# Four-layer convolution block: weights of two mixing steps in one transfer, spectra as the stationary operand, single buffers, results stored by image, weight preparation split over three engines

## What is computed

```
x_ft = jnp.fft.rfft2(x, norm='ortho')
xt = x_ft[:, :, :56, :57]
w = jax.lax.complex(weight[:, :, :56, :57, 0], weight[:, :, :56, :57, 1])
out_ft = jnp.einsum('bchw,cohw->bohw', xt, w)
...
return jnp.fft.irfft2(out_ft_full, s=(H, W), norm='ortho')
```

## Time and profile before

| | |
|---|---|
| Time, median of 3 runs | 11767.94 us (11765.45 to 11776.15) |
| Time of the profiled execution | 11769.75 us |
| Its span | 11767.7 us |
| Mixing stage, first matmul to last | 1629.3 to 2627.4 us |
| Busy in the span | PE 88%, DVE 67%, ACT 51%, POOL 33% |

### The profile page before, as it was taken

The page is one execution under the profiler, slowest core; times in us unless marked ns, Lnnn a source line. Parts: engine busy times, 40 slices in busy tenths (PEclk is TensorE's granted clock), DMA queues, the critical chain, the costliest instruction groups (busy, mean ns, idle before and its releaser), DMA issues.

```text
span 11767.7 us, 292004 instructions
## 1 busy us (share of the span) xinstructions
PE 10317.4 (88%) x120871; PEld 9151.4 (78%) x120871; DVE 7890.7 (67%) x13708; ACT 5969.8 (51%) x7016; POOL 3941.8 (33%) x3304
## 2 busy tenths in 40 slices
PE   7989978874999889999999999999889999999996
PEld 5777777774888878888888888888778888888885
DVE  7777722115677777777777777777677777777775
ACT  4666621112555555555555555555555555555553
POOL 0000000002444444444444444444444444444442
PEclk9999988886999999999999999999999999999996
DMA  8999999982111121111111111111121111111100
GB/s 206 239 241 241 245 210 233 235 214 53 28 39 36 44 45 36 36 37 37 39 36 39 36 39 37 39 39 36 42 46 37 36 36 38 36 39 38 37 22 17
DMA packets 1001966, 947.34 MB, mean 81 GB/s; under 512 B 592800, under 2 KB 937872, under 8 KB 980944
## 3 DMA queue, kind: packets, MB, share of 16 engines
q1 hardware_dynamic: 972048, 708.59, 28.4%
q0 software_dynamic: 28608, 220.21, 5.0%
HBM read 605.77 MB, written 322.96 MB: 79 GB/s over the span
## 4 chain that ended last, share of the span: by engine, by line
PE 38%; DVE 17%; ACT 7%; issue 7%; POOL 5%; DMA 1%; SPq 0%; DVEq 0%; POOLq 0%; ACTq 0%
PE c_ps L1029 24%; PE c_ps L1100 3%; POOL c_cube L1740 3%; PE c_ps L1178 3%; PE c_ps L1113 2%; PE c_ps L1165 2%; DVE c_v L1542 2%; ACT c_xp L1286 2%; DVE c_xp L1506 2%; DVE c_bn L1486 2%; DVE c_s L1605 2%; DVE c_xr L1524 2%; ACT c_sq L1349 1%; ACT c_xp L1226 1%; DVE c_qt L1580 1%
## 5 line engine op out<-in xcount | busy, mean ns | idle before, releaser
L1029 PE MATMUL c_ps<-c_xp,c_wst 128*128 128x224 f16 x45696 | 4911.4, 265 | 154.8 <-DVE c_xp L1506 154.8
L1029 PEld LDWEIGHTS c_ps<-c_xp,c_wst 128*128 128x128 f16 x45696 | 4366.7, 98 | 634.9 <-issue 415.6
L1715 POOL TENSOR_TENSOR c_xr<-c_sm,c_xr 128x448 f32<-128x448 f32 x448 | 704.0, 1572 | 2217.0 <-DVE c_xr L1524 2216.9
L1740 POOL TENSOR_TENSOR c_cube<-c_sq,c_qk 128x896 f32<-128x896 f32 x448 | 928.3, 2093 | 1194.3 <-ACT c_sq L1340 1194.3
L1317 ACT ACTIVATE c_qt<-c_ps 128x896 f32<-128x896 f32 x224 | 205.8, 919 | 2042.1 <-PE c_ps L1121 2042.1
L1275 ACT ACTIVATE c_tn<-c_xr,c_nrm 64x448 f32<-64x448 f32 (+1 forms) x832 | 956.0, 1153 | 57.0 <-DVE c_xp L1506 27.0
L1100 PE MATMUL c_ps<-c_wqkv,c_xn 64*128 64x192 f32 x6272 | 791.2, 367 | 200.5 <-DVE c_v L1542 193.0
L619 PE MATMUL b_ps<-b_xs,b_wt 64*64 64x64 f32 x6384 | 774.2, 294 | 207.0 <-DVE b_xj L595 160.8
L1286 ACT ACTIVATE c_xp<-c_tn 128x1080 f16<-128x1080 f32 (+1 forms) x544 | 572.2, 1063 | 737.4 <-DVE c_tn L1499 733.6
L1506 DVE TENSOR_TENSOR c_xp<-c_tn,c_xp 128x1080 f16<-128x1080 f32 (+1 forms) x544 | 664.1, 1230 | 271.7 <-ACT c_xp L1286 270.7
L1100 PEld LDWEIGHTS c_ps<-c_wqkv,c_xn 64*128 64x128 f32 x6272 | 516.3, 195 | 384.5 <-DVE c_v L1542 287.2
(11 more groups left out here) (158 smaller groups left out, 17750.2 us busy)
## 6 DMA issues: line engine op xcount, KB each, us to landing
b_wt<-in_L_conv_weight SPq DMA_DIRECT2D x56, 2048.0 KB, 21.8
a_xc<-in_x SPq DMA_DIRECT2D x64, 1568.0 KB, 21.4
x<-a_x1s POOLq DMA_DIRECT2D x64, 1568.0 KB, 12.1
a_xh<-x SPq DMA_DIRECT2D x64, 1568.0 KB
c_xr<-x SPq DMA_DIRECT2D x224, 448.0 KB, 4.0
out<-c_xr SPq DMA_DIRECT2D x448, 224.0 KB, 3.1
b_xs<-xf SPq DMA_DIRECT2D x28, 2048.0 KB, 24.5
yf<-b_ys POOLq DMA_DIRECT2D x28, 2048.0 KB, 12.1
```

Of the source, the lines that this page charges most:

```text
L1029: ins = pe.matmul(sums(c, p), wst[:, ws, pr, FIRST_TAP[p] + k].rearrange("p q o -> p (q o)"), xp[:, xs, PLANE[kind] + f, row:row + CROWS, ...
L1715: pool.tensor_tensor(here, apart(sm[:, half]).unsqueeze(1).to_broadcast([P, 2, CROWS, QW]), here, ALU.add).then_inc(s.added, 1)
L1740: pool.tensor_tensor(cube[:, :, k].rearrange("p q r c -> p r q c"), sq[:, :, :, k], qk[:, :, :, k], ALU.mult).then_inc(done, 1)
```

## The change

- The weights of two steps (`m`, 14 pairs) come in one transfer for each half: 4.2 MB with pieces of 1024 bytes. `wt` still has two buffers, each now of two steps. For that the rows of a step are re-numbered (a permutation of the constant `fwd_h`; the amount of work is the same).
- The spectra `xs` have one buffer. `load_x(k)` waits until `turn` has read the spectra before (`turned`), and stands in SP's program behind the weights of its pair.
- `turn` makes three parts (minus imaginary, real, imaginary) for each frequency with the images innermost, `xt`, with three DVE instructions that read `xs` in steps of 512 bytes and write without gaps. `xt` has two buffers.
- PE takes 64 columns of `xt` as the stationary operand, and the 64 outputs' weights, 1024 bytes apart, as the moving one. Number and sizes of the matmuls are the same.
- The results `ys` are laid out by output channel and have one buffer: the copies of step k + 1 wait for the stores of step k. A step is stored with four transfers of 32 partitions (32 images, 16 KB each) into `yf`, now (image, real or imaginary, frequency row, channel, 64). The places of two neighbouring images are 1792 KB apart there.
- Stage C loads an image's mixed spectra with two transfers without gaps, half the bytes of before, and `ys` is half as large.
- In `prepare_weights` ACT makes the high f16 part, and DVE the low one; of the 8 slices of `spread` DVE makes 5 (125 instructions), and POOL 3, with 49 instructions of 384 elements.

SP's program in the mixing stage, before: one step of the loop's body, two transfers of weights (L528) and one of spectra (L531); a row "ISA" in front holds the waits.

The diff, without the parts that only rename:

```diff
-        wt = sb("wt", [P, 2, C, FP // 2, 2])
-        xs = sb("xs", [P, 2, B, FP // 2, 2])
-        xj = sb("xj", [P, 2, B, FP // 2, 2])
-        ys = sb("ys", [P, 2, B, FP // 2, 2])
-        loaded = [sem("loaded0"), sem("loaded1")]
+        wt = sb("wt", [P, 2, C, 2, FP // 2, 2])
+        xs = sb("xs", [P, B, FP // 2, 2])
+        xt = sb("xt", [P, 2, KW, 3, B])
+        ys = sb("ys", [P, C, FP // 2])
+        w_loaded = [sem("w_loaded0"), sem("w_loaded1")]
+        x_loaded = sem("x_loaded")
         turned = sem("turned")
         mixed = [sem("mixed_low"), sem("mixed_high")]
         copied = [sem("copied_low"), sem("copied_high")]
-        stored = [sem("stored0"), sem("stored1")]
+        stored = sem("stored")
         padded = sem("padded")
-        PER = min(BANK // (2 * B), 8)
+        PER = BANK // C
         GROUPS = -(-KW // PER)
         block = ctx.enter_context(nc.Block())
         @block.sync
         def _(sp):
-            def load(k, odd):
-
+            def load_w(m, odd):
                 for half in range(2):
-                    if above_zero((k - 1) * GROUPS):
-                        sp.wait_ge(mixed[half], (k - 1) * GROUPS)
+                    if above_zero((m - 1) * 2 * GROUPS):
+                        sp.wait_ge(mixed[half], (m - 1) * 2 * GROUPS)
                         sp.nop(nofuse=True)
-                src = weight.rearrange("c o (k two) w r -> two k c o w r", two=2)
+                src = weight.rearrange("c o (m two u) w r -> two m c o u w r", two=2, u=2)
                 for half in range(2):
-                    sp.dma_start(wt[C * half:C * half + C, odd],
-                                 src[half, bass.ds(k, 1)].rearrange("k c o w r -> (k c) o (w r)")
-                                 ).then_inc(loaded[odd], 16)
-                sp.dma_start(xs[:, odd], xf[bass.ds(k, 1)].rearrange("k p b f -> (k p) (b f)")).then_inc(loaded[odd], 16)
-
-            load(0, 0)
-            load(1, 1)
-            with sp.Fori(0, KP // 2 - 1) as t:
+                    sp.dma_start(wt[C * half:C * half + C, odd].rearrange("p o u w r -> p o (u w r)"),
+                                 src[half, bass.ds(m, 1)].rearrange("m c o u w r -> (m c) o (u w r)")
+                                 ).then_inc(w_loaded[odd], 16)
+
+            def load_x(k):
+                if above_zero(k):
+                    sp.wait_ge(turned, k)
+                    sp.nop(nofuse=True)
+                sp.dma_start(xs[:], xf[bass.ds(k, 1)].rearrange("k p b f -> (k p) (b f)")).then_inc(x_loaded, 16)
+
+            load_w(0, 0)
+            load_x(0)
+            load_w(1, 1)
+            for k in range(1, 4):
+                load_x(k)
+            with sp.Fori(0, KP // 4 - 1) as t:
                 for odd in range(2):
-                    load(2 * t + (2 + odd), odd)
+                    load_w(2 * t + (2 + odd), odd)
+                    for u in range(2):
+                        load_x(4 * t + (4 + 2 * odd + u))
         @block.gpsimd
...
             pool.memset(ys[:], 0.0).then_inc(padded, 1)
-            def store(k, odd):
+            def store(m, u):
+                k = 2 * m + u
                 for half in range(2):
                     pool.wait_ge(copied[half], (k + 1) * GROUPS)
                     pool.nop(nofuse=True)
-                pool.dma_start(yf[bass.ds(k, 1)].rearrange("k p b f -> (k p) (b f)"), ys[:, odd]
-                               ).then_inc(stored[odd], 16)
+                for half in range(2):
+                    for r in range(2):
+                        rows = slice(C * half + B * r, C * half + B * r + B)
+                        there = yf[:, r, bass.ds(4 * m + (2 * half + u), 1)]
+                        pool.dma_start(there.rearrange("b k o w -> (b k) (o w)"), ys[rows].rearrange("p o w -> p (o w)")
+                                       ).then_inc(stored, 16)
             store(0, 0)
-            store(1, 1)
+            store(0, 1)
             with pool.Fori(1, KP // 2) as t:
-                for odd in range(2):
-                    store(2 * t + odd, odd)
-            for odd in range(2):
-                pool.wait_ge(stored[odd], 16 * (KP // 2))
+                for u in range(2):
+                    store(t, u)
+            pool.wait_ge(stored, 64 * KP)
         def take(eng, copy, half, between):
...
             def body(k, odd):
-                if above_zero(8 * (k - odd)):
-                    eng.wait_ge(stored[odd], 8 * (k - odd))
+                if above_zero(64 * k):
+                    eng.wait_ge(stored, 64 * k)
                 for g in range(GROUPS):
                     lo, hi = g * PER, min(g * PER + PER, KW)
                     eng.wait_ge(mixed[half], k * GROUPS + (g + 1))
-                    copy(ys[C * half:C * half + C, odd, :, lo:hi].rearrange("p b w r -> p w b r"),
-                         ps[C * half:C * half + C, 4 * half + g % 4, 0:2 * B * (hi - lo)].rearrange(
-                             "p (w b r) -> p w b r", b=B, r=2)).then_inc(copied[half], 1)
+                    rows = slice(C * half, C * half + 2 * B)
+                    copy(ys[rows, :, lo:hi].rearrange("p o w -> p w o"),
+                         ps[rows, 4 * half + g % 4, 0:C * (hi - lo)].rearrange("p (w o) -> p w o", o=C)
+                         ).then_inc(copied[half], 1)
                     if g == GROUPS // 2:
...
             def turn(k, odd):
-                dve.wait_ge(loaded[odd], 24 * (k + (2 - odd)))
+                dve.wait_ge(x_loaded, 16 * (k + 1))
                 for half in range(2):
                     if above_zero((k - 1) * GROUPS):
                         dve.wait_ge(mixed[half], (k - 1) * GROUPS)
-                dve.tensor_scalar(xj[:, odd, :, 0:KW, 0], xs[:, odd, :, 0:KW, 1], -1.0, None, ALU.mult)
-                dve.tensor_copy(xj[:, odd, :, 0:KW, 1], xs[:, odd, :, 0:KW, 0]).then_inc(turned, 1)
+                by_freq = xs[:, :, 0:KW].rearrange("p b w r -> p r w b")
+                dve.tensor_scalar(xt[:, odd, :, 0], by_freq[:, 1], -1.0, None, ALU.mult)
+                dve.tensor_copy(xt[:, odd, :, 1], by_freq[:, 0])
+                dve.tensor_copy(xt[:, odd, :, 2], by_freq[:, 1]).then_inc(turned, 1)
...
         def _(pe):
-            def body(k, odd):
-                pe.wait_ge(loaded[odd], 24 * (k + (2 - odd)))
+            def body(m, odd, u):
+                k = 2 * m + u
+                pe.wait_ge(w_loaded[odd], 16 * (m + (2 - odd)))
                 pe.wait_ge(turned, k + 1)
                 for g in range(GROUPS):
                     lo, hi = g * PER, min(g * PER + PER, KW)
@@ -612,20 +631,24 @@
                             pe.nop(nofuse=True)
                     for f in range(lo, hi):
-                        at = 2 * B * (f - lo)
-                        for r, src in ((0, xs), (1, xj)):
+                        at = C * (f - lo)
+                        for r in range(2):
                             for half in range(2):
                                 rows = slice(C * half, C * half + C)
-                                ins = pe.matmul(ps[rows, 4 * half + g % 4, at:at + 2 * B], wt[rows, odd, :, f, r],
-                                                src[rows, odd, :, f], start=(f == lo and r == 0),
+                                ins = pe.matmul(ps[C * half:C * half + 2 * B, 4 * half + g % 4, at:at + C],
+                                                xt[rows, u, f, 1 - r:3 - r].rearrange("p r b -> p (r b)"),
+                                                wt[rows, odd, :, u, f, r], start=(f == lo and r == 0),
                                                 stop=(f == hi - 1 and r == 1), skip_group_check=True)
                                 if f == hi - 1 and r == 1:
                                     ins.then_inc(mixed[half], 1)
-            body(0, 0)
-            body(1, 1)
-            with pe.Fori(1, KP // 2) as t:
+            def step(t):
                 for odd in range(2):
-                    body(2 * t + odd, odd)
+                    for u in range(2):
+                        body(2 * t + odd, odd, u)
+
+            step(0)
+            with pe.Fori(1, KP // 4) as t:
+                step(t)
...
+SPREAD_DVE = 5
...
+        def turned_taps(ky):
+            return ps[0:C, 3 * (ky % 2):3 * (ky % 2) + 3].rearrange("c b x -> c (b x)")[:, 0:TAPS * C].rearrange(
+                "c (k o) -> c k o", k=TAPS)
+
+        def place(part, ky, q):
+            pr, rp = divmod(ky + q, 2)
+            return to["wst"][C * rp:C * rp + C, part, pr, :, q]
...
+            pool.wait_ge(loaded, 16 * len(LOADS))
+            pool.nop(nofuse=True)
+            shape = [P, WS - SPREAD_DVE, P]
+            for t in range(25):
+                there = to["spread"][:, SPREAD_DVE:WS]
+                here = there if t == 0 else term[:]
+                pool.tensor_tensor(here, taps[:, t].unsqueeze(1).to_broadcast(shape),
```

(38 more changed lines are left out.)

5 lines of the change are left out of this document (4 added, 1 removed).

## The result

The changed kernel takes **11,731.8 us** (median of 10 runs, 11,718.8 to 11,739.6) against 11,764.1 of the kernel before, measured beside it: ratio 0.9972, 95% interval 0.9963 to 0.9980. It is 0.28% faster. The forecast was 11,805, slower; the time lies in the forecast's range (11,700 to 11,950), the sign was wrong.

What follows compares the result with a forecast made beforehand. The prediction took the mixing stage's transfer queue, empty during `turn`, as the bound: +79 there, -28 preparation, -3.5 and -10 at C's start, +37 us on 11769.75, giving 11,805 us (range 11,700 to 11,950).

Steps and rivals of the forecast that it cites:

- for later images these loads have nobody waiting: Stage C: the halved loads of spectra save time only for image 0 (10 us), nothing for later images.
- the rest of C at nothing: Stage C behind its start: no term in the sum, so no change of time expected.
- `turn` at 8.6 us: Mixing stage, once a pair: three instructions take 8.6 us (lower bound 3.4) with the queue empty; a pair takes 75.7.
- the first rival: Mixing stage: `turn` costs 3.4 us, total put at 11,728 us; decides from about 5.5 us downwards; chance 32%.
- Start and end of the stage: Mixing stage: first `turn` at 1648.0 us, step 1's to 1709.1, step 26 at 2642, end 2717 against 2638.2.
- Copies at nothing: Mixing stage: copies into `ys` with gaps, even at twice their time 1.4 us of a group's 4.0, hidden.
- Stores: Mixing stage rival: stores land after 18.6 us, each us over 24.6 costs two a pair; 11,911 us at 29; chance 15%.
- the pace of 126 ns: PE in the mixing stage: a pair of records in one half keeps 126 ns, between half and double that.
- The rival of a dear moving operand: PE in the mixing stage: gaps cost double, a step takes 57.6 us, PE is the bound, total 12,376; chance 8%.
- Preparation, -28: Weight preparation: split -11 us, `spread` -19, and 2 added for DVE and POOL at once, 28 us shorter.
- The term of 2 us for DVE and POOL at once: Weight preparation: 2 us added for both engines working in SBUF at the same time.
- Start of C, -13.5: Start of stage C: halved memset of `ys` saves 3.5 us, halved spectra of image 0 save 10.

Runs made afterwards that it cites:

- `code_back`: The changed kernel with 111 idle instructions more in PE's program, in the weight preparation: 11,773.3 us, 1.0005 of the kernel before.
- `turn_long`: The changed kernel with the third instruction of `turn` run three times over: 11,788.4 us, 1.0018 of the kernel before.
- `pool_later`: The changed kernel with POOL's share of `spread` starting only when DVE has laid out the kernel's parts: the preparation stage takes 119.5 us.
- `spread_undone`: The changed kernel with all of `spread` on DVE again, the split still with ACT: the preparation stage takes 123.6 us, 5.3 more than the changed kernel.

## Why the prediction was wrong

- **The step that failed** is "for later images these loads have nobody waiting", and with it the rest of C at nothing. It is true of the loads: with the same light loads, `code_back` has the old 8941.3 us. But the change also makes the program of PE's mixing loop twice as long and so moves all of stage C in its pieces of 256 instructions: 52 us in the two profiles, 34 to 39 against the other kernels with that PE program, and by the medians some 40 (`code_back` 11,773 against 11,732). No term of the sum spoke of it, although the kernel before has waits for nothing else ("issue") in its rows. That the time lies in the range is luck: `turn` (-45), the conflict of DVE and POOL (+10) and C (-41) together take the sum of 11,805 to 11,729, and a range made for `turn` and the stores happened to be wide enough.
- **`turn` at 8.6 us**: it took 5.1, between my bounds of 3.4 and 8.6, and close below the 5.5 from which I had the first rival decide (cheap `turn`, faster). But that rival did not bring the gain either: with `turn` at 5.1 the sum is 45 us lower, 11,760, which is no difference. That "faster" came out is, for this rival, luck. The mechanism was right: with the very 8.6 us I had assumed (`turn_long`) a pair takes 76.3 us, forecast 75.7, and the stage 1129, forecast 1119. Only the size was off. I took it from L1478 for its 16 bytes an element, but DVE reads an f32 every 512 bytes at 0.95 ns each (1.73 us for 1824). What makes L1478 dear is something else, and was not looked into. 3.5 us at each of 13 turns make 45; step 26 begins 1004 us after the first transfer, 40 earlier than forecast.
- **Start and end of the stage**: first `turn` at 53.0 us after the first transfer (forecast 49.9), `turn` of step 1 at 99.9 (102.4), from step 26 to the next block 77 (75). Weights alone on the queue run at 205 GB/s (2042 to 2048 us; forecast 200 to 205).
- **Copies at nothing**: they grew from 635 to 922 ns (DVE) and from 548 to 953 (ACT). PE waits 27 us for them in the whole stage, beside 193 for `turn`; since the queue sets the pair, I take this for hidden, and no run varies the copies alone. **Stores**: the next step's first copy begins 11.5 to 15.0 us after the issue, in all steps, under the forecast 18.6 and the limit of 24.6. That rival fell.
- **PE's operands**: I kept the pace of 126 ns. It is 111 (eight matmuls start 0.444 us apart, 0.504 before), LDWEIGHTS' median 150 ns, MATMUL 285 against 294. The rival of a dear moving operand fell. By the rule of the Trainium skill that I cited for it (SBUF — State Buffer, "Door 1: The DMA port swizzle"), the gaps would now cost in the moving operand; no such cost shows here.
- **Preparation, -28**: the split -12.8 (forecast -11) and `spread` -18.3 (-19) were right. The term of 2 us for DVE and POOL at once is 12, shown by `pool_later` and `spread_undone`. The Trainium skill (SBUF — State Buffer, "Terms") calls it a port pair that the two lock for a whole instruction, with ACT and PE apart from it. The trace agrees in kind: the copy of the parts goes from 576 ns (L773 before) to 1288 (L829), while L862, which has PSUM as an input and runs beside POOL too, takes 1281, against 1283 before.
- **Start of C, -13.5**: the memset -3.4 as forecast, from the load's issue to PE 12.2 us in place of 25.8, so -13.6, not -10.
- **A row misread**, without effect on the sum: the 410 GB/s at 2810 us are not the spectra of stage C, which had landed by then (PE, which waits for them, starts at 2808.4), but the loads of x behind them, which have 128 partitions too. The spectra are the 177 GB/s.

With `turn` at 5.1 and the conflict at 12 the sum had been 11,770, no difference, which is what `code_back` measures (11,773). Part of this agreement is luck: the terms would be +34, -18 and -13.5, and +41, -16 and -18 were measured, whose errors partly cancel. So the change in the mixing stage itself is a loss of 41 us there, against 34 us won in the two stages behind it.

## What to carry to other kernels

Where a change alters the length of an engine's program, nothing behind it stays as it was: look for "issue" in the waits of the engine that bounds a later loop, and measure the change once more with idle instructions that put that loop back on its old place, before any of the gain is put down to the change. A price taken from the nearest row needs that row's own reason: two rows that both read with gaps may not share what makes one of them dear. A queue that is empty now can only be filled by another order if the buffer of what is to be moved up is free by then: look first when its last reader ends. And a delay that is easy to see in a trace, as the late store here, need not be what costs the time: find a run that has the one without the other.
